# One routing set for the tokens of batches 0 and 1, and result rows summed by VectorE: a two-layer gated cross-attention and mixture-of-experts kernel

## The reference, cut to what matters

```python
x = x + tanh(g_xattn[0]) * L0_xattn(layernorm(x), ctx)   # 16 heads, int8-coded q and output projections
# L0_ffn, on layernorm(x):
shared = (silu(gu[:, :704]) * gu[:, 704:]) @ se_down_w.T * sigmoid(x @ shared_gate_w.T)
weights, sel = top_k(softmax(x @ gate_w.T), 4)
for e in range(60):                                      # every token's 4 chosen experts count
    sparse += cw[:, e] * ((silu(x @ w1[e]) * (x @ w3[e])) @ w2[e])
x = x + tanh(g_ffn[0]) * (shared + sparse)
x = x + tanh(g_xattn[1]) * L1_xattn(layernorm(x), ctx)   # decayed mean of ctx, one summary row per batch, layernorm
x = x + tanh(g_ffn[1]) * L1_ffn(layernorm(x))            # sigmoid router, 8 experts, 2 per token, shared expert
```

## Time and profile before

| what | value |
|---|---|
| median of three runs | 628.03 us |
| profiled execution, its own time | 631.99 us |
| span of the profile | 630.2 us |
| PE busy | 544.6 us, 86% |
| DVE busy | 363.7 us, 58% |
| ACT, POOL busy | 241.5 us, 226.6 us |
| attention, up to the last score eviction | to about 211 us |
| rest of the routing, shared expert's first half | to about 272 us |
| experts of L0 | 272.6 to 441.8 us |
| stretch between the experts | 443.8 to about 535 us |
| L1's experts, then the end | 559.5 to 611.1 us, then to 630.2 us |

### The profile page before, as it was taken

One profiled execution on the slowest core, in us unless ns is written; L12 is line 12 of the kernel. 1 busy time (PEld: TensorE's weight loads), 2 busy tenths in 40 slices (PEclk: granted clock), 3 DMA queues, 4 the chain that ended last, 5 costly groups with the idle time before them and its releaser, 6 DMA issues. The chain is left out here.

```text
span 630.2 us, 11162 instructions
## 1 busy us (share of the span) xinstructions
PE 544.6 (86%) x3510; PEld 367.8 (58%) x3510; DVE 363.7 (58%) x1172; ACT 241.5 (38%) x477; POOL 226.6 (36%) x280
## 2 busy tenths in 40 slices
PE   3799999998799779989969999998898968749975
PEld 1466566666566554466657777766456644427754
DVE  6687678675886777146784555544156454215532
ACT  2368778876778412012322333322122242003320
POOL 2211023040116254513334777763132341753440
PEclk9989999998999898999999999999799979959998
DMA  8910720891001028339876999993430200828926
GB/s 287 323 35 3 234 91 3 269 365 55 1 3 72 2 77 254 121 111 279 281 236 198 265 285 279 289 277 120 144 132 0 71 0 1 301 99 250 319 88 200
DMA packets 61445, 101.12 MB, mean 160 GB/s; under 512 B 7881, under 2 KB 37373, under 8 KB 61264
## 3 DMA queue, kind: packets, MB, share of 16 engines
q1 hardware_dynamic: 53808, 87.47, 44.9%
q0 software_dynamic: 7584, 13.02, 6.0%
HBM read 70.25 MB, written 38.57 MB: 173 GB/s over the span
## 5 line engine op out<-in xcount | busy, mean ns | idle before, releaser
L626 POOL DMA_INDIRECT token_y<-stage,y_row x78 | 76.7, 983 | 114.7 <-ACT stage L1511 104.8
L1958 PE MATMUL bank<-stage 128*128 128x352 f32 x312 | 110.2, 477 | 3.5 <-DMA stage<-in_w 2.5
L844 DVE CUSTOM_DVE_ANT_0 stage<-bank,stage 128x512 f32<-128x512 f32 x128 | 80.8, 687 | 30.0 <-PE bank L1722 29.3
L1413 ACT ACTIVATE stage<-bank 128x512 f32<-128x512 f32 x128 | 73.7, 597 | 42.0 <-PE bank L1736 41.4
L1976 PE MATMUL bank<-stage,e_hT 88*128 88x256 f32 x312 | 81.7, 384 | 1.0 <-DVE e_hT L1194 1.0
L1736 PEld LDWEIGHTS bank<-ident,stage 128*128 128x128 f32 x512 | 57.0, 144 | 38.9 <-issue 32.5
L1501 ACT ACTIVATE e_act<-bank 128x176 f32<-128x176 f32 x78 | 24.8, 317 | 140.3 <-PE bank L1958 140.3
L1736 PE MATMUL bank<-ident,stage 128*128 128x128 f32 x512 | 73.8, 285 | 5.0 <-ACT stage L1413 4.6
L1976 PEld LDWEIGHTS bank<-stage,e_hT 88*128 88x128 f32 x312 | 59.9, 193 | 23.0 <-DVE e_hT L1194 1.5
L1861 PE MATMUL bank<-xnT,sh_in 128*128 128x512 f32 (+2 forms) x144 | 71.1, 649 | 2.3 <-issue 2.0
L1958 PEld LDWEIGHTS bank<-stage 128*128 128x128 f32 x312 | 54.7, 195 | 24.2 <-issue 3.3
(11 more groups left out here) (238 smaller groups left out, 710.3 us busy)
## 6 DMA issues: line engine op xcount, KB each, us to landing
stage<-in_w SPq DMA_DIRECT2D x30, 704.0 KB, 8.2
stage<-in_w SPq DMA_DIRECT2D x48, 352.0 KB, 4.5
stage<-sorted_x SPq DMA_DIRECT2D x39, 272.0 KB, 6.2
sorted_x<-zeros SPq DMA_DIRECT2D x4, 2040.0 KB, 13.3
extra_x<-zeros SPq DMA_DIRECT2D x4, 1088.0 KB, 12.2
stage<-token_y SPq DMA_DIRECT2D x8, 512.0 KB, 4.6
sorted_x<-zeros SPq DMA_DIRECT2D x4, 816.0 KB, 13.5
stage<-in_w SPq DMA_DIRECT2D x18, 176.0 KB
```

Source lines behind the costliest of these rows:

```text
L626: gp.indirect_dma_start(out=y_dram[y.n][:, :], out_offset=bass.IndirectOffsetOnAxis(y_row[:, t:t + 1], 0), in_=e_y[:, t % NY, :], in_offse ...
L844: V.tensor_tensor_reduce(out=z_sb[:, s % 2, j, :], in0=bank[j][:], in1=mask[:, b % 2, k // 4, :], scale=-1.0, scalar=BIG, op0=ALU.add, op1 ...
L1413: A.activation(pT[:, s % 2, j].rearrange("p t n -> p (t n)"), bank[4 + j % 2][:], ACT.Exp, scale=1.0 if j < ON_ACT else -1.0).then_inc(exp ...
L1958: last = M.matmul(bank[2 + u % 2][:, 0:2 * I_EXP], xgT[:, u, c, :], w13[:, u, c, :], start=(c == 0), stop=(c == CC - 1))
```

## The change

Two independent edits. **Routing:** `FIRST = 1` names the first set that is routed; it holds the four tiles of batches 0 and 1. In batch 2 of attention nothing is routed any more (only the tokens are normalised and turned, as before); in batch 3 every routing operation runs on four tiles in place of two. Batch 0's scatters move from inside the loop to behind it, and `power` now stands between batch 0's and batch 1's scatters. **Summing:** `sum_rows` is gone from PE in both layers; `combine` adds the K rows of two tiles at a time to `x` on DVE, all operands in SBUF, and SP's loads wait for `combined` in place of `summed`. PE no longer waits for `combined` before `turn_mixed(0)` and before L1's first `up_shared`.

```diff
+        FIRST = 1
+        def part_tiles(c):
+            return range(0 if c == FIRST else c * QT, (c + 1) * QT)
...
-            JOBS += [(j, c) for j, c in here if 0 <= c < B]
+            JOBS += [(j, c) for j, c in here if (FIRST if j in ("lg", "ps") else 0) <= c < B]
...
                     if i >= NY:
-                        sp.wait_ge(f["summed"], i - NY + 1)
+                        sp.wait_ge(f["combined"], i - NY + 1)
...
                     code_o(b - 1)
-                if b > 2:
-                    dispatch_part(b - 3)
...
             settle(B - 2)
+            dispatch_part(0)
+            power(var_o, B)
             dispatch_part(1)
-            power(var_o, B)
             dispatch_part(2)
...
-                if k == 4 and b > 1:
-                    route_logits(b - 2)
+                if k == 4 and b == FIRST + 2:
+                    route_logits(FIRST)
...
-                if k == 6 and b > 1:
-                    route_pick(b - 2)
+                if k == 6 and b == FIRST + 2:
+                    route_pick(FIRST)
...
-            def combine(y, tiles):
-                f = fs[y.n]
-                for i in tiles:
...
-                    dve.wait_ge(f["summed"], i + 1)
-                    V.tensor_tensor(x_sb[:, i, :], bank[sum_bank(y, i)][:, 0:D], x_sb[:, i, :], ALU.add).then_inc(f["combined"], 1)
+            def combine(y, g):
+                f, t, u = fs[y.n], g * QT, g * QT % NY
...
+                for i in range(t, t + QT):
+                    dve.wait_ge(y_ld[i % NY], rows_loaded(y, i))
+                x = x_sb[:, t:t + QT, :]
+                for k in range(y.K - 1):
+                    step.done(V.tensor_tensor(x, yk[:, u:u + QT, k, :], x, ALU.add))
+                V.tensor_tensor(x, yk[:, u:u + QT, y.K - 1, :], x, ALU.add).then_inc(f["combined"], QT)
...
             ffn(L0)
-            up_shared(L0, NSH)
-            up_shared(L0, NSH + 1)
-            sum_rows(L0, range(2))
-            up_shared(L0, NSH + 2)
-            sum_rows(L0, range(2, 4))
-            for m in range(NSH + 3, 2 * NSH):
+            for m in range(NSH, 2 * NSH):
                 up_shared(L0, m)
             pe.wait_ge(fs[0]["up_free"], 2 * NSH)
             down_shared(L0, range(4, 6))
-            sum_rows(L0, range(4, 6))
             turn_mixed(0)
             down_shared(L0, range(6, 8))
-            sum_rows(L0, range(6, 8))
             turn_mixed(1)
-            pe.wait_ge(fs[0]["combined"], NT)
```

More of the change, by code:

```diff
@@ L278, in build @@
                 "bounced", "even_rows", "odd_rows", "index_ready", "late_step",
-                "shared_added", "summed", "combined", "extra_slots") if (k not in ("late_step", "log_full", "pos_full", "h_made", "shared_added") if y.extra else k[0:2] not in ("o_", "ox", "ex"))})
+                "shared_added", "combined", "extra_slots") if (k not in ("late_step", "log_full", "pos_full", "h_made", "shared_added") if y.extra else k[0:2] not in ("o_", "ox", "ex"))})
             for i in range(PAIRS):
@@ L316, in head, with part_view, at_part, part_slice @@
             return cc, par, cc * 8 + 2 * j + par
+        FIRST = 1
+        def part_tiles(c):
+            return range(0 if c == FIRST else c * QT, (c + 1) * QT)
+        def part_view(c, buf):
+            n = len(part_tiles(c))
+            return buf[:, 0:n]
+        def at_part(c):
+            n = len(part_tiles(c))
+            flat = summary[:].rearrange("p b d -> p (b d)") if c == FIRST else tmp[:, 6:8, :].rearrange("p t d -> p (t d)")
+            return flat[:, 0:n * KM * EM].rearrange("p (t k e) -> p t k e", t=n, k=KM)
+        def part_slice(c):
+            return slice(part_tiles(c)[0], part_tiles(c)[-1] + 1)
+        def parts_done(c):
+            return c - FIRST + 1
         SUBS = QT * 4
@@ L928, in route_pick @@
             def route_pick(c):
-                f, K, t = fs[0], L0.K, slice(c * QT, (c + 1) * QT)
-                for i in range(c * QT, (c + 1) * QT):
+                f, K, t, n = fs[0], L0.K, part_slice(c), len(part_tiles(c))
+                for i in part_tiles(c):
                     step.add(V.max(top8[:, i, :], probs[:, i, :]))
                 step.wait()
-                for i in range(c * QT, (c + 1) * QT):
+                for i in part_tiles(c):
                     step.add(V.max_index(idx8[:, i, :], top8[:, i, :], probs[:, i, :]))
@@ L1297, in add_rows @@
                 def add_rows(g):
-                    combine(L0, range(g * QT, (g + 1) * QT))
+                    combine(L0, g)
                     dve.wait_ge(fs[0]["combined"], (g + 1) * QT)
@@ L1348, in _ @@
             experts(L1)
-            combine(L1, range(NT))
+            for g in range(B):
+                combine(L1, g)
         @block.scalar
@@ L1446, in _ @@
                         take_codes("co", b - 1, QT)
-                if k == 4 and b > 1:
-                    route_exp(b - 2)
+                if k == 4 and b == FIRST + 2:
+                    route_exp(FIRST)
             back(B - 1, 1)
@@ L1688, in gate_logits @@
                 dst = bank[job_bank("lg", c)]
-                for i in range(QT):
-                    t = c * QT + i
+                for i, t in enumerate(part_tiles(c)):
                     for cc in range(CC):
@@ L1696, in places @@
             def places(c):
-                pe.wait_ge(fs[0]["mem_ready"], c + 1)
+                pe.wait_ge(fs[0]["mem_ready"], parts_done(c))
                 bank_free("ps", c)
                 dst = bank[job_bank("ps", c)]
-                for i in range(QT):
-                    t = c * QT + i
+                for i, t in enumerate(part_tiles(c)):
                     o = dst[:, i * 64:i * 64 + EM]
@@ L1796, in _ @@
                     turn_q(b + 1)
-                if k == 7 and b > 1:
-                    places(b - 2)
+                if k == 7 and b == FIRST + 2:
+                    places(FIRST)
                 turn_z(s, 2)
@@ L1806, in _ @@
                     turn_x(b - 2)
-                if k == 3 and b > 1:
-                    gate_logits(b - 2)
+                if k == 3 and b == FIRST + 2:
+                    gate_logits(FIRST)
                 if k == 4 and b:
@@ L1863, in up_shared @@
                 last.then_inc(f["up_full"], 1)
-            def sum_rows(y, tiles):
-                f = fs[y.n]
-                for i in tiles:
-                    pe.wait_ge(y_ld[i % NY], rows_loaded(y, i))
-                    if y.n and i > 3:
-                        pe.wait_ge(f["combined"], i - 3)
-                    if y.own and i in (2, 3):
-                        pe.wait_ge(f["combined"], i - 1)
-                    for k in range(y.K):
-                        last = M.matmul(bank[sum_bank(y, i)][:, 0:D], ident[:], yk[:, i % NY, k, :], start=(k == 0), stop=(k == y.K - 1))
-                    last.then_inc(f["summed"], 1)
             def turn_mixed(g):
@@ L1882, in turn_mixed @@
                     pe.wait_ge(xT_ev, g)
-                else:
-                    pe.wait_ge(fs[0]["combined"], 4)
                 for c in range(CC):
@@ L2056, in _ @@
             ffn(L1)
-            sum_rows(L1, range(NT))
 def layout(i):
```

59 lines of the change are left out of this document (29 added, 30 removed).

## The result

In 20 executions of each, the changed kernel has a median of 628.27 us (622.77 to 634.55) and the kernel before 631.62 us (627.25 to 638.51). The ratio is 0.9941, 95% interval 0.9914 to 0.9968, so 3.7 us are gained (2.0 to 5.4). The forecast of a gain of 4.9 us lies in that interval; the predicted time of 623.0 us, and its range up to 628, do not hold 628.27, since 628.03 us, the median of three executions, was no typical time of the kernel before.

The account below looks back on a forecast made before the run. PE was busiest, but bounds were read by stage: PE's waits for DVE's routing, PE's sums between the experts, loads and sums at the end. -2.9 - 0.8 - 1.2 = -4.9 us from 628.03 gave 623, range 618 to 628.

Parts of the forecast that it names:

- The sum: Whole kernel: -2.9 - 0.8 - 1.2 = -4.9 us, giving 627.1 from the profiled execution, 623.1 from the median of 628.03.
- Attention, batch 2: Attention's batch 2, rid of routing: PE's waits, gate logits and late evictions go, only `turn_x` stays; -7.1 us.
- Batch 3: Attention's batch 3, routing four tiles: +1.07 us for gate logits on PE, +2.45 for pick and softmax on DVE.
- POOL: 0: POOL behind attention's loop: eight more scatters fit its idle 9.82 us, so the sorted tokens are not late; 0 us.
- The clock at attention's end: Attention's end: PE idle some 3.9 us, then a slower clock; +0.7 us, between 0 and +2.9.
- Between the experts: Between the expert loops: sums moved to DVE give -3.2 us, clock fall behind PE's pause +2.4; together -0.8.
- A: Rival, attention's end and between the experts: PE stays at 2.4 GHz, 3.1 us more won, 620.0 us; chance 0.20.
- C: Rival, same two places: clock falls fully, +2.9 for 0.7 and +3.4 for 2.4, 626.3 us; chance 0.18.
- Rival B: DVE's additions between the experts and at the end: each takes 1.31 us, +0.62 more, total 633 us; chance 0.10.
- The end: Kernel's end: loads issued earlier after DVE's additions, last addition 626.4 against 627.60; -1.2 us, bounds -0.3 and -2.

Follow-up runs that it names:

- run 7: The changed kernel, but PE again sums groups 0 and 1 of the first layer, DVE the rest; 0.9861 against the kernel before.
- run 3: The kernel before with only the routing edit, sums left on PE; 0.9952 against the kernel before.
- run 9: The changed kernel with the root for batch 3's tokens on POOL behind six scatters in place of eight; 626.94 us in a single execution.
- run 5: The changed kernel with useless identity products (10, 18, 20) queued in PE's three pauses between the experts; 0.9978 against the kernel before.
- run 6: The changed kernel with 5, 9 and 13 useless identity products in PE's three pauses between the experts; 0.9897 against the kernel before.
- run 12: The changed kernel with PE summing groups 0 and 1, end loads at once, PE's slot products late, useless products in the two pauses left; 617.98 us, 0.9784.
- Run 8: The changed kernel with all eight loads of the second layer's expert rows issued at once; 0.9944 against the kernel before, end 13.99 us.
- run 10: The changed kernel with PE's slot products behind the step's last turns and values, DVE's slots later too; 0.9856 against the kernel before.
- run 4: The kernel before with only the summing edit, DVE summing the rows, routing as before; 0.9976 against the kernel before.

## Why the prediction was wrong in its number and right in its gain

**The step that failed** is in "The sum": "the same difference from the median gives 623.1". It moved the sum to a base of 628.03 us, and twenty executions of the kernel before have a median of 631.62; less 4.9 that is 626.7, 1.6 us from 628.27. Two of the three executions behind 628.03 lay at the low end of a spread of 11 us, and the range had terms for costs of the change, none for the base. The profiled execution's own sum, 627.1, would have stood 1.2 us from 628.27, but by luck: its 631.99 happened to lie 0.4 us from that median.

Where part of the spread comes from: the loop took 166.9 to 172.6 us over ten profiles of kernels that don't differ in it. PE's waits in the loop, of the kernel of run 7 (loop 167.08) and of run 3 (172.64), sum, times, longest in us:

```profile
PE bank L1985 <- DMA stage<-in_w: 1.2, 2, 0.6
```
```profile
PE bank L1981 <- DMA stage<-in_w: 4.4, 6, 1.0
```

The experts' weights come late by 3.2 us more in the one; the mean granted clock of the loop is 0.99 in both. Why the weights came late there, and what the other 2.4 us are, was not settled.

**Attention, batch 2** (-7.1): right, -7.11. It takes 46.25 us, to 0.01, in each of the eleven profiles with the edit, and 53.22 to 53.36 in the three without.

**Batch 3** (+3.52): 3.08. Pick and softmax, put at +2.45, cost 1.93 in PE's wait. The wide comparison and reduction grew as told (+0.50 and +0.80 for +0.5 and +0.8); too high were search, index and cast (+0.9, measured 0.62) and softmax (+0.25; from its start to the next score 1.88 us, 1.75 before).

**POOL: 0** is a mis-sized term, with the place wrong: 0.7 us. The sorted tokens were not late, but the root for batch 3's rows stood behind the scatters, and 0.52 us of slack, which the kernel before had there, went; run 9 gave it back. A further term stands at nothing without a reason: `places` itself on four tiles. Its products take 0.50 us (209.34 to 209.84) ahead of the next transposes, and took 0.21 before (213.89 to 214.10), 0.3 us more. PE before:

```profile
214.10 1.88 PE L1736 MATMUL bank<-ident,stage 128*128 128x128 f32 x8
```

**The clock at attention's end** (+0.7): near 0. PE's clock fell there before the change too, and the transposes and values behind the mask took 4.57 us before and 4.62 now. PE's windows of before and then of the changed kernel:

```profile
214.00:218.00 4.00, 4.00 (x63) 0.57 0.00 0
```
```profile
208.00:210.00 2.00, 0.66 (x11) 0.50 0.00 0
210.00:212.00 2.00, 2.00 (x17) 0.50 0.00 0
212.00:214.00 2.00, 2.00 (x56) 0.65 0.00 0
```

The errors cancel, which is luck: -2.8 in place of -2.9.

**Between the experts** (-3.2, clock +2.4): the steps came as told: pauses of 2.81 and 4.84 us (the second told as 5.1, the first only implied by the times given), the last product of the half 2.79 us late, counted from the second (471.80 - 448.24, before 475.31 - 454.54; +1.05 and +2.4 told), and from it to the last statistics 19.80 us in place of 23.92. The clock took 1.7 us where +2.4 stood, or 3.4 where it fell more often, so the stretch gives -1.33 or +0.35. The forecast lay between rivals A (the clock holds) and C (it falls fully), and so did the first outcome; the second comes near C. The Trainium skill (TensorE: Matmul & The Clock Gate, section "HAM oscillation — how this bites in real kernels") tells of just such cold bursts behind waits. Runs 5, 6 and 12 agree, since the last chunk takes 3.65 us in place of 5.34, and the first shared chunk 3.60 in place of 5.96, where PE has work in the pause.

**Rival B** is out: the 24 additions of `combine` (L1307, L1308) took 0.684 to 0.693 us. The other row of 1.31 us came again (465.65, above), again beside POOL:

```profile
465.14 1.27 POOL L670 TENSOR_TENSOR stage<-x_sb,rows 128x512 f32<-128x512 f32 x1
```

**The end** (-1.2): -0.15 in the first profiles, less than its smaller bound of -0.3. The eight profiles with DVE's sums and loads in pairs took 15.85 to 16.40 us, the three with PE's sums 16.50, 16.50 and 17.69, so the size is known only as 0.1 to 1.8. The first pair of additions came when told (done 8.7 us behind PE's last product, told 8.5), but a pair of loads takes 3.4 and 4.2 us from the last addition ahead of it to the next (612.31 to 615.69, 614.36 to 618.51), where one load's 3.32 had been taken from the earlier trace rows; the bound of -0.3 had named the cause. Run 8 shows that the wait for buffers was the bound.

Added up from the changed kernel's two profiles (against the first of before) the gain is 3.1 to 4.3 us: 2.8, then 1.33 or a loss of 0.35, then 0.15 or 0.62. That the forecast's 4.9 lies in the measured interval owes something to its width.

## What to carry to other kernels

Work that only keeps PE busy can be worth its time: taken away ahead of other PE work, it leaves a pause, and the clock behind the pause can take back part of the gain, or all of it. Move work off PE where PE is what ends last (groups 2 and 3 here), and leave it where PE would wait. And take the base of a forecast from more than three executions, or widen the range by its spread: it was 627 to 639 us here, more than twice the gain that was forecast.

## What the runs showed that was not expected

A short pause can be followed by half clock, and a longer one need not be. Pauses of 1.00, 1.42 and 1.25 us, with at most 1.5 us of products between them, were followed by a granted clock of 0.5 (run 10), and five products of no use in each of the last two kept it at 1.0 there (run 12). Behind the pause of 2.81 us between the experts the chunk took 3.70 us in the first profile, and 5.17 behind one of 2.80 in run 4. The stages of attention repeat from one execution to the next, to 0.04 us with the routing edit and to 0.15 us without it, so an edit of 0.7 us can be read from one profile where twenty times can't tell it.
